# A gated cross-attention block: scores by pairs of half-array matmuls in place of one full-array matmul

## The reference

```
def xattn(x, context):                    # 16 heads of 32
    q = split_heads(x @ Wq)               # (2, 16, 2048, 32)
    k = split_heads(context @ Wk)         # (2, 16, 77, 32)
    v = split_heads(context @ Wv)
    scores = einsum('bhid,bhjd->bhij', q, k) * 32 ** -0.5
    attn = softmax(scores)                # over the 77 context tokens
    return merge_heads(einsum('bhij,bhjd->bhid', attn, v)) @ Wo

x = x + tanh(g_xattn) * xattn(layernorm(x), ctx)
x = x + tanh(g_ffn) * ffn(layernorm(x))   # two up products to 1408, silu, one down product
```

## Time and profile before

| | us |
|---|---|
| median of 3 runs | 640.35 |
| lowest and highest | 639.74, 644.17 |
| the profiled execution, its own time | 639.99 |
| its span, first to last instruction | 638.2 |
| TensorE busy in the span | 619.3 |
| VectorE busy | 509.9 |
| ScalarE busy | 352.3 |

### The profile page before, as it was taken

One profiled execution on the slowest core, in us unless ns is written; L12 is line 12 of the kernel. 1 busy time (PEld: TensorE's weight loads), 2 busy tenths in 40 slices (PEclk: granted clock), 3 DMA queues, 4 the chain that ended last, 5 costly groups with the idle time before them and its releaser, 6 DMA issues. The chain is left out here.

```text
span 638.2 us, 12704 instructions
## 1 busy us (share of the span) xinstructions
PE 619.3 (97%) x3891; PEld 468.8 (73%) x3912; DVE 509.9 (80%) x954; ACT 352.3 (55%) x512; POOL 197.6 (31%) x416
## 2 busy tenths in 40 slices
PE   7899999999999999999999996999999999899997
PEld 6689999999999999999999995444444444444544
DVE  6588788898988889899988666788888888866764
ACT  4264656666566766656664343555555554355653
POOL 7122243333333333323421212111111110057775
PEclk9999999999999999999999997999999999999999
DMA  8738522222232223222411000276455110099623
GB/s 305 204 84 267 133 59 68 54 62 49 58 66 58 66 58 66 73 41 77 97 43 49 25 0 1 49 240 226 134 138 197 33 26 8 4 342 410 265 107 124
DMA packets 85206, 69.61 MB, mean 109 GB/s; under 512 B 64915, under 2 KB 67373, under 8 KB 85165
## 3 DMA queue, kind: packets, MB, share of 16 engines
q1 hardware_dynamic: 79752, 52.27, 29.7%
q10 hardware_dynamic: 5413, 16.84, 7.4%
HBM read 32.48 MB, written 21.36 MB: 84 GB/s over the span
## 5 line engine op out<-in xcount | busy, mean ns | idle before, releaser
L1302 ACT ACTIVATE sb_silu<-ps_g,sb_sgu 128x512 f32<-128x512 f32 x88 | 60.5, 688 | 72.0 <-PE ps_g L1389 43.8
L1389 PE MATMUL ps_g<-sb_xqT,sb_wgu 128*128 128x512 bf16 x344 | 89.3, 379 | 1.0 <-DVE sb_xqT L1345 0.6
L1389 PE MATMUL ps_u<-sb_xqT,sb_wgu 128*128 128x512 bf16 x346 | 89.4, 379 | 0.3
L590 ACT COPY sb_pT<-ps_p 128x512 f32<-128x512 f32 (+1 forms) x96 | 46.5, 521 | 70.4 <-PE ps_p L1005 70.4
L1360 DVE SCALAR_TENSOR_TENSOR sb_h<-ps_u,sb_sgu,sb_silu 128x512 f32<-128x512 f32 (+1 forms) x88 | 66.0, 750 | 19.4 <-PE ps_u L1389 18.7
L949 PE MATMUL ps_q<-sb_xT_hi,sb_wq_hi 128*128 128x256 f32 x256 | 78.0, 305 | 2.2 <-DVE sb_q_lo L685 2.2
L1016 PE MATMUL ps_o<-sb_vblk,sb_pT 128*128 (+4 forms) x640 | 79.1, 271 | 0.0
L1016 PEld LDWEIGHTS ps_o<-sb_vblk,sb_pT 128*128 128x128 f32 (+1 forms) x640 | 76.8, 191 | 0.5
L951 PE MATMUL ps_q<-sb_xT_hi,sb_wq_lo 128*128 128x256 f32 x256 | 72.3, 282 | 0.0
L950 PE MATMUL ps_q<-sb_xT_lo,sb_wq_hi 128*128 128x256 f32 x256 | 72.2, 282 | 0.0
L1595 PE MATMUL ps_z<-sb_wdT,sb_hq 128*128 128x512 bf16 x324 | 71.7, 381 | 0.3
(11 more groups left out here) (218 smaller groups left out, 1344.1 us busy)
## 6 DMA issues: line engine op xcount, KB each, us to landing
h_spill<-sb_h SPq DMA_DIRECT2D x4, 2816.0 KB, 9.1
sb_h<-h_spill ACTq DMA_DIRECT2D x16, 704.0 KB, 6.6
out_dram<-sb_wgu SPq DMA_DIRECT2D x31, 256.0 KB, 2.3
sb_x<-in_x_dram ACTq DMA_DIRECT2D x1, 4096.0 KB, 18.0
sb_w_in<-in_L_ffn_w_gate_dram SPq DMA_DIRECT2D x11, 256.0 KB, 2.6
sb_w_in<-in_L_ffn_w_up_dram SPq DMA_DIRECT2D x11, 256.0 KB, 2.6
sb_x<-in_x_dram SPq DMA_DIRECT2D x2, 1024.0 KB, 15.2
sb_x<-in_x_dram SPq DMA_DIRECT2D x2, 512.0 KB, 5.2
```

Source lines behind the costliest of these rows:

```text
L1302: act.activation(silu[(j * KI + i) % 2][:, :, :].rearrange("p t n -> p (t n)"), p_g[(j * KI + i) % 2][:, :], ACT.Silu, scale=sgu[:, i:i + ...
L1389: last = pe.matmul(banks[(j * KI + i) % 2][:, :], wgu[:, what, k, i * P:(i + 1) * P], xqT[j][:, k, :], start=(k == 0), stop=(k == KD - 1))
```

## The change

A chunk's four heads are split over the two halves of the array. Rows 0 to 63 with 154 columns of keys (two heads, the upper left part of the block diagonal) go as one matmul to bank 0 of `p_s`, rows 64 to 127 with the other 154 columns as another to bank 1, and chunk i takes the columns from 154i in both banks. Each of the three products of a chunk is such a pair, so a half has twelve matmuls in six pairs, with 128 columns of queries as the stationary operand of each. Bank j now holds heads 0 and 1, or 2 and 3, of both chunks of a half, so the order of the eight heads in a half changes: `head_at` gives the head at each place. V is spread in that order, and Wo's rows are loaded in it, by four DMAs in place of one (the wait for it is 64 in place of 16). The loop of `tile_slots` has three rounds in place of four; slots 16 to 19 are written out, on every engine, and in the scores the batch is a constant (0 in the loop, which now covers slots 4 to 15).

```
+RT2 = 2
+HT = HG // RT2
+TW = HT * M
+PT = P // RT2
+
+def head_at(place):
+    j, rest = divmod(place, HH // RT2)
+    i, r = divmod(rest, HT)
+    return HG * i + HT * j + r
...
-                    with eng.Fori(1, 5) as i:
+                    with eng.Fori(1, 4) as i:
                         for t in range(4):
                             slot(i * 4 + t, t)
-                    for n in range(20, NT + 4):
+                    for n in range(S // P, NT + 4):
                         slot(n, n % 4)
...
                         eng.dma_start(vblk[r0 - P * k:r1 - P * k, b, :, SLOT0[k] + h - heads_of(k)[0], :],
-                                      v_sb[b][r0 - M * h:r1 - M * h, h:H:HH, :]).then_inc(l_v[b], 16)
+                                      v_sb[b][r0 - M * h:r1 - M * h, head_at(h):H:HH, :]).then_inc(l_v[b], 16)
...
-                    sp.dma_start(wo_raw, weights(Wo)).then_inc(l_wo, 16)
+                    for f in range(2):
+                        for i in range(2):
+                            sp.dma_start(wo_raw[i * PT:(i + 1) * PT, 2 * f:2 * f + 2, :],
+                                         Wo.rearrange("(f i j e) n -> f i e j n", f=2, i=2, j=2)[f, i])                              .then_inc(l_wo, 16)
...
-                            act.wait_ge(l_wo, 16)
+                            act.wait_ge(l_wo, 64)
...
-                        b = n // (S // P)
+                        b = n // (S // P) if isinstance(n, int) else 0
                         rows = slice(t % 2 * P, (t % 2 + 1) * P)
                         for i in range(2):
                             g = 2 * half + i
                             qh, ql = q_hi[t // 2][:, g, rows], q_lo[t // 2][:, g, rows]
-
-                            def keys(a):
-                                return a[:, span(b), g, :].rearrange("p a n -> p (a n)")
-                            s = p_s[:, i, 0:GW]
-                            pe.matmul(s, qh, keys(k_hi), start=True, stop=False)
-                            pe.matmul(s, qh, keys(k_lo), start=False, stop=False)
-                            last = pe.matmul(s, ql, keys(k_hi), start=False, stop=True)
+                            for q, k, first, end in ((qh, k_hi, True, False), (qh, k_lo, False, False),
+                                                     (ql, k_hi, False, True)):
+                                for j in range(RT2):
+                                    part = slice(j * PT, (j + 1) * PT)
+                                    last = pe.matmul(p_s[:, j, i * TW:(i + 1) * TW], q[part],
+                                                     k[part, b, g, j * TW:(j + 1) * TW],
+                                                     start=first, stop=end, skip_group_check=True)
                         last.then_inc(t_s, 1)
```

## The result

| | us |
|---|---|
| the changed kernel, median of 7 runs | 649.28 |
| lowest and highest | 646.34, 649.55 |
| the kernel before, beside it, median of 7 runs | 643.56 |
| ratio | 1.011, 95% interval 1.0085 to 1.0136 |
| the profiled execution, its span | 647.5 |

The change makes the kernel 1.1% slower; the forecast was 1.2% faster, from 640.35 us. The times of both kernels fall into two groups some 3 us apart, before at 640 and 643.6, after at 646.4 and 649.4, and of the changed kernel the upper group has the lower mean granted clock (0.987 to 0.989 against 0.992 to 0.995). Within a group the change costs 6.4 and 5.8 us. Experiment 11 takes away one stretch of the lower clock; what decides between the groups stays open.

A forecast was written before the change was run, and what follows sets the result against it. The prediction took TensorE's gapless stream in the attention stage as the bound. From the median of 640.35 us, -10.8 for loads side by side and +3.2 for borders gave -7.6, so 632.7 us, range 626 to 675.

The forecast's parts named there:

- What bounds the kernel: Attention stage: TensorE has no gap, so each nanosecond its stream gives up is one of the kernel, while VectorE's 13% hold.
- Term 1, columns: Score matmuls: 154 columns take 0.072 us, less than a weight load's 0.112 us, so columns do not set the pace.
- Term 2, loads side by side: Score bursts: the two halves' weight loads run at once, 0.112 us a pair, gaining 0.34 us a tile, 10.8 us in all.
- the other bound: Score bursts: the halves' loads run one after the other, losing 1.01 us a tile, 32 us; as a rival, chance 0.22.
- Term 3, borders: Four changes a tile between full array and halves: 0.08 us each entry to scores, 0.01 each exit, 3.2 us in all.
- The drain rival: The array empties at each change of division: +9.7 us, 650 us, or 657 with uncovered loads; chance 0.17.
- Who is next, and the other edits: VectorE has 1.4 us of room a slot, so the gain lands in full; written-out slots and Wo's four DMAs cost 0.
- The narrow form of the rounded operands: Score matmuls: rival that 154-column rounded operands fall to 0.26 us a pair, +46 us, 686 us; chance 0.06.

The follow-up runs named there:

- Experiment 11: Changed kernel with ScalarE's copy of the second queries moved ahead of its five DMA issues that spread V: 645.22 us, ratio 1.0087.
- 2: Changed kernel with each of its 24 matmuls a tile over all 128 rows, so the array is never divided: 670.67 us, ratio 1.047.
- 3: Changed kernel with the middle product of each chunk over the full rows, giving six borders in each half in place of two: 701.49 us, ratio 1.095.
- 4: Changed kernel with both matmuls of a pair on rows 0 to 63: 688.09 us, ratio 1.074.
- 8: Each half's scores computed twice: full-array scores with the other edits, 693.88 us, ratio 1.0817; changed kernel with pairs, 690.05 us, ratio 1.0763.
- 5: Changed kernel with pairs in half 0 alone, half 1 having the full matmuls of the kernel before: 645.39 us, ratio 1.0076.
- 6: Changed kernel with pairs in half 1 alone, half 0 having the full matmuls of the kernel before: 645.46 us, ratio 1.0079.
- 12: Kernel before with the last two probability transposes of the previous tile moved ahead of the scores of half 1: 639.51 us, ratio 0.9989.
- q_first_join_full: Kernel before with the queries' copy ahead of the DMA issues and the last two probability transposes ahead of half 1's scores: 635.19 us, ratio 0.992.
- unroll_only: Kernel before with slots 16 to 19 written out and the batch of the scores a constant: 641.84 us, ratio 1.0028.

## Why the prediction was wrong

- **What bounds the kernel**: right. TensorE's stream has no gap in the attention stage, and the large changes of the slot (2, 3, 4, 8) came out in the time within 1.3 us of slot times 32. The small ones (5, 6, 12) show in the slot; their times are off by 1.3 to 3.1 us, as much as the start moves.
- **Term 1, columns**: right that they don't decide; 154 columns on the full array go at 0.11 us, the load's pace (2).
- **Term 2, loads side by side**: right, and it was the riskiest choice. 0.112 us a pair, the second load 3 ns behind the first; the pairs gave 0.352 us a tile where 0.34 stood. The price of the other bound was right too: loads in file cost 12.03-11.11 = 0.92 us a slot where 1.01 stood. The Trainium skill's page TensorEngine Tiling (Array Packing), section Key Properties, says that different tiles can execute LdWeights and Matmul in parallel. By the 3 ns between the two loads of a pair the trace agrees.
- **Term 3, borders**: this is the step that failed. "I keep the 0.08 that half 1 pays and charge the same at the entry of half 0, and 0.01 at each exit: 0.10x32 = 3.2 us." The changed kernel pays 0.153+0.147 at half 0 and 0.187-0.086+0.147 at half 1: 0.548 us a tile, 17.5 us, not 3.2 (the entry at half 1 by itself, 0.10 more than before, stood at 0). The rows taken were borders between kinds of work on an undivided array, which say nothing of a change of division; between far bounds (0 and 20.5 us, with uncovered loads 27) I had put the value beside the lower. The gain of the pairs themselves was 0.352 us a tile (17.5-6.3 = 11.2 us), so the sum is +6.3 where -7.6 stood.
- **The row that was there.** "The trace of before never changes the division and so can't confirm it" was wrong, or at least unchecked. The one-row matmuls of line 1143, whose loads I had quoted for their pace, stand between full ones and pay at both ends. Their row ends in "[0.17 <-issue]", an idle time without a wait, and the matmuls of the kernel before around them are:

```profile
10.00 0.60 PE L1139 MATMUL ps_p<-sb_identf,sb_o_sb 128*128 128x128 f32 x4
10.53 0.38 PE L1143 MATMUL ps_o<-sb_wgu 1*128 1x4 f32 x2
10.84 0.60 PE L1112 MATMUL ps_q<-sb_identb 128*128 128x512 bf16 x2
```

Four transposes 0.11 us apart from 10.00 end their starts at 10.33; the next start comes at 10.53, 0.20 us on, exactly the 0.202 of the changed kernel's exits. Behind the two one-row records (10.66 the second) the next comes at 10.84, 0.18 us on, and its load starts 0.20 us behind the load before it, where the pace is 0.11. Read so, the rows of before hinted at 0.09 us in each direction for the wait alone; four times 32 of them are 11.5 us, the whole gain. It is a hint and no more: one such passage in a profile (each has it, with the same distances), with other kinds of work and other types around it, and no experiment here varied it.

- **The drain rival** (chance 0.17) is the one that the runs bear out, in its place and sign: +9.7 us forecast, +6.3 measured. That its 650 us lies so near the 649.28 is luck: it was reckoned from 640.35, a time of the lower group, and there the changed kernel takes 646.4. Its price of 0.16 us for a lost overlap is close to a border's 0.15, but the parts are others: about 0.09 for the wait and 0.06 for the load that isn't made in advance. The sum came out smaller mainly since half 1 had paid for its entry before. Experiment 3 has 0.157 us for each further change. The same page and section of the Trainium skill say that changing the tiling mode drains the TensorE. The runs agree that each change has a price; that it is a drain is the likely reading of them, and not shown. I gave the rule too little weight: the same section was believed for the loads.
- **Who is next, and the other edits**: no new wait, right; VectorE's room was not needed. The four DMAs cost 0, right. The written-out slots cost 0.28% alone, where 0 stood; the cause is open, and within the two groups of times of the changed kernel it doesn't show.
- **Small slips**: without borders the sum is 640.35-10.8 = 629.6 us, where the forecast's own range began at 628; and the 11.04 us of a slot is an average that has the first, shorter slots in it, where an ordinary one takes 11.106.

The range, 626 to 675 us, held the time; the direction was wrong.

## What to carry to other kernels

Two matmuls in the two halves of the array do run at once, loads too, so a pair costs what one load costs, here 0.11 us; but each change between full and half use costs 0.15 us (0.10 more than before where the entry was already dear), so count the borders before the columns. With six pairs between two borders the saving of 0.028 us a pair was 0.17 against 0.30; with twelve pairs, 0.34 against the same 0.30, the pairs just won. Where a stream must alternate, order the neighbours so that fewer borders are left, which was not run here, or leave it undivided.

## What was not expected of the hardware

- Matmuls written in the order upper, upper, upper, lower, lower, lower rows ran in pairs, as fast as when written alternately (burst of 0.835 us for 0.828).
- A border costs the same with a 512-column matmul of rounded operands ahead of it (0.089 us beyond its pace) as with transposes of 128 columns behind it (0.090).
- The narrow form of the rounded operands is not dear: 154 columns go at 0.11 us, on the full array and in the halves.
- TensorE's clock stood at the lower level for 3.4 to 10.2 us, from 27 to 30 us on, in 13 of the 16 profiles; without it are the profile of before and the two of the swap (`q_first_pairs`, `q_first_join_full`), where the wait for the queries near the start was 0.7 us. The length of that wait doesn't explain it alone: before had 2.2 us and no such stretch, `unroll_only` 2.1 us and 6.8 us of the lower clock.
